# A decoder stack in one kernel: the rotary halves of its keys, its last batch and its two ends rearranged

## The chip, the cores and the metric

The kernel runs on one core of one Trainium2 chip. The metric is the device time of one execution in microseconds (us). Four compute engines and a queue appear in this text: PE (TensorE, matmuls; PEld is its weight load), DVE (VectorE), ACT (ScalarE), POOL (GpSimd), and SP (SyncE), which here only issues transfers.

## What is computed

Six layers in a row on x (8, 256, 128), each followed by `x = _layernorm(x + layer(x))`:

```
L0_attn   windowed self-attention, 16 heads of 8, band of 64, relative bias
L0_xattn  cross-attention, x against ctx_1024 (8, 512, 128), 16 heads of 64
L0_ffn    layernorm, ternary weights, activations rounded to 8 bits
L1_attn   recurrence over 256 steps: state = tanh(state @ A.T + u_t @ B.T) + sp_t
L1_xattn  linear attention with 16 heads of 8, against ctx_1024
L1_ffn    fp8 quantised product with one scale for the whole tensor
```

The change is mostly about one piece of L0_xattn, the keys:

```
k, v = jnp.split(ctx @ Wkv, 2, axis=-1)
x1, x2 = (k[..., :32], k[..., 32:])                   # per head of 64
k = jnp.concatenate([x1 * cos - x2 * sin, x2 * cos + x1 * sin], axis=-1)
attn = softmax(clip(q @ k.T / 8, -11, 11))
```

## The kernel before

Each of the five engines runs its own instruction stream, written out by hand, and waits on semaphores that the others raise. There is no scheduler: the order of the calls in the five `@block` functions is the order on the engines. The order of work is:

**Setup** (to 57.7 us). SP loads all weights. The windowed self-attention of batch 0 runs in full (`first_scores`, `first_turn`, `first_weigh`), and the weights of the cross-attention are split in a high and a low part, so that a product of them takes three matmuls (`split_mm`, L1757 to L1759): ACT makes the high parts (`split_high`), POOL the low ones (`split_low`, L697).

**Eight batches.** A batch is a loop over 8 head pairs p (a pair is two heads of 64, one matmul operand of 128 rows). On PE a pair is two score units of 8 matmuls (`unit`, L2132), the values and the sum of the pair before (`values_of` L2056, `sum_of` L2064), and jobs that prepare later pairs in spare PSUM banks: "keys a", "keys b", "queries", "values 0", "values 1" (`prep_targets`, `number_jobs`; the bank alternates between `bank_p` and `SECOND_BANK[p]`). ACT takes the exponentials of a unit (L1006). DVE clamps them (`clamp`, L1470), takes the reciprocal of the sums and the product for the pair before (`attended`, L1372 and L1373). POOL adds the four quarters of the probabilities (L731, L733, L734) for the sum. Six *slots* per pair hold pieces of the next batch's self-attention, on every engine (`self_attention(b + 1, slot)`).

The keys of pair p + 2 are made thus. PE multiplies `wk_s` ("keys a") and, with weights whose 32-row halves are swapped, `wkx_s` ("keys b"), each with 512 columns of context. DVE multiplies the first bank by `cos_t` into `k_cos` (L1314) at the start of the pair and the second by `sin_t` into `k_sin` (L1316) behind `attended` and the second clamp. POOL adds them into `kr` (`rotate`, L641). `k_cos` has one buffer, so the next key product waits for that addition (`kr_ready`).

**Last batch** (about 711 to 781.5). It has no slots; `beside_last_batch(p)` prepares the FFN and the matrices of the recurrence. Behind it PE runs `output_of_last`, then `sum_of(63)`.

**Transition** (to 815.4). Last norms, quantisation of the FFN's activations (`quantize_f`), the FFN's product, norm (`normalize_x3`), turns of x3 and `begin_z(0)`, `begin_z(1)`, the inputs of the first recurrence steps.

**Recurrence** (255 steps, L2260 on PE and L1055 on ACT). `late_work(t)` puts the rest of the FFN and of the inputs between steps (`LATE_Z = 29`: 27 thirds of a product, one per step from step 29 on), `window(k, i)` the layer L1_xattn for the 16 steps before, `keep_clock` matmuls without use.

**End** (964 to 1021.9). The last windows, the peak of x5 over all tokens, quantisation, the last product and norm. POOL adds the bias there (`add_bias`, L785), DVE normalises (`normalize`, L1189).

Of the kernel before, what the change touches and what calls it, by code (L numbers as in the profile page):

```python
# [28 lines left out]
S = 512  # L29
# [58 lines left out]
def prep_targets(p, last):  # L88

    target = {}  # L90
    if p == PAIRS - 1:
        return {} if last else {"keys a": 1, "values 0": 0, "values 1": 0, "queries": 0, "keys b": 1}
    if p + 2 < PAIRS or not last:
        target["keys a"] = (p + 2) % PAIRS
    target["queries"] = p + 1
    if p + 2 < PAIRS or not last:
        target["keys b"] = (p + 2) % PAIRS
    if p % 2 == 1:
        target["values 0"] = target["values 1"] = (p + 1) // 2
    return target  # L100
# [3 lines left out]
FIRST_JOBS = {("keys a", 0): 0, ("keys b", 0): 0, ("values 0", 0): 0, ("values 1", 0): 0, ("keys a", 1): 1,  # L104
              ("keys b", 1): 1, ("queries", 0): 0}
# [3 lines left out]
def number_jobs():  # L109
# [3 lines left out]
    def add(key, kind, target, second):  # L113
        nonlocal bank
        bank = second if second and bank == "p" else "p"
# [26 lines left out]

SELF_NORMS = 3
# [10 lines left out]
LATE_Z = 29  # L154
HALF_ROWS = P // 2


def n(b, per, k):

    return b * per + k  # L160
# [19 lines left out]
def decoder(nc, a, out):  # L180
    with ExitStack() as ctx:
# [16 lines left out]
        prep_bank = {"p": bank_p, "o0": o0_bank, "d2": bank_d2}  # L198
# [17 lines left out]
        wkx_s = sb("wkx_s", [P, 2, INNER], F32R)  # L216
# [57 lines left out]
        k_cos = sb("k_cos", [P, S])  # L274
        k_sin = sb("k_sin", [P, S])
# [119 lines left out]
        rel_ready = sem("rel_ready")  # L395
        qkv_in = sem("qkv_in")
# [31 lines left out]
        weights_split = sem("weights_split")  # L428
        kv_centred = sem("kv_centred")
# [10 lines left out]
        lat_ready = sem("lat_ready")  # L440
        kr_ready = sem("kr_ready")
# [35 lines left out]
        trig_nat = prob1[:, 6, :].rearrange("p (t k d) -> p t k d", t=2, k=KB)  # L477
# [6 lines left out]
        FIRST_LOADS = 5  # L484
# [3 lines left out]
        def _(sp):  # L488
            loads = {rel_in: 0, qkv_in: 0, first_in: 0, ctx_cols_in: 0, keep_in: 0, split_in: 0, weights_in: 0}
# [13 lines left out]
            load(w_nat[:, 0:3, :], a["L0_attn_w_qkv"].rearrange("(k p) c -> p k c", p=P), signal=qkv_in)  # L503
            load(w_nat[:, 3, :], a["L0_attn_w_proj"], signal=qkv_in)
            sp.dma_start(cb[:, :, :], a["ctx_1024"][0].rearrange("(k p) d -> p k d", p=P)).then_inc(ctx_in, 16)
            load(trig_nat[:, 0], a["L0_xattn_cos"].rearrange("(k p) d -> p k d", p=P), signal=first_in)
            load(trig_nat[:, 1], a["L0_xattn_sin"].rearrange("(k p) d -> p k d", p=P), signal=first_in)
            load(w_l1kv[:, 0:D], a["L1_xattn_wk"], signal=first_in)
            load(w_l1kv[:, D:2 * D], a["L1_xattn_wv"], signal=first_in)
            row("L0_attn_b_proj", b_proj, signal=first_in)  # L510

            sp.wait_ge(d_free, 1)
            sp.dma_start(scratch, rel_row).then_inc(scratch_out, 16)
            col("L0_xattn_ln_ctx_g", CTX_G, signal=ctx_cols_in)
            col("L0_xattn_ln_ctx_b", CTX_B, signal=ctx_cols_in)
            load(keep[:, :, :], a["mask_BxS2_ff1"].rearrange("b (k p) -> p b k", p=P), slow=True, signal=keep_in)
            sp.wait_ge(scratch_out, 16)
            for j in range(G):
                sp.dma_start(bias_mask[:, j:H:G, :], rows(scratch, (1, P), j * SCRATCH, [(G * SCRATCH, G), (1, BAND)])
                             ).then_inc(bias_in[j], 16)  # L520
            load(wkv_nat, a["L0_xattn_Wkv"], signal=split_in)
            load(wq_nat, a["L0_xattn_Wq"], signal=split_in)
            row("L1_xattn_ln_gamma", l1_g)
# [16 lines left out]
            assert loads == {rel_in: 1, qkv_in: 2, first_in: FIRST_LOADS, ctx_cols_in: 2, keep_in: 1, split_in: 2,  # L540
                             weights_in: SETUP_LOADS}, loads

            def load_next(b, src):

# [3 lines left out]
                sp.dma_start(xb[:, :, :], a["x"][src].rearrange("(k p) d -> p k d", p=P)).then_inc(x_in, 16)  # L548

# [7 lines left out]
            for b in range(1, B):  # L557
                load_next(b - 1, b)

            sp.wait_ge(y_full, B - 1)  # L560
            for k, name in ((M_WI, "L1_attn_Wi"), (M_WS, "L1_attn_Ws"), (M_WO, "L1_attn_Wo"), (M_A, "L1_attn_A"),
                            (M_B, "L1_attn_B"), (M_C, "L1_attn_C"), (M_FFN0, "L0_ffn_weight"),
                            (M_FFN1, "L1_ffn_weight")):
                sp.dma_start(mats[:, k, :], a[name]).then_inc(mats_in, 16)

            x4_of_batch = x4_dram.rearrange("k (i b) d -> b k i d", b=B)
            for k in range(1, WINDOWS + 2):
# [26 lines left out]
        def _(pool):  # L594
# [3 lines left out]

            g.memset(ones[:, :], 1.0)
# [4 lines left out]
            g.memset(ident[:, :], 0.0)  # L604
# [3 lines left out]
            g.affine_select(out=ident[:, :], in_=ident[:, :], compare_op=ALU.not_equal, fill=1.0, base=0,  # L608
# [1845 lines left out]
```

## Time and profile before

| | us |
|---|---|
| median of three runs (lowest, highest) | 1025.55 (1023.43, 1025.63) |
| the profiled execution | 1023.58 |
| its span in the profile | 1021.9 |
| setup | 57.7 |
| a steady batch (418.13 to 511.17) | 93.04 |
| the recurrence, one step | 0.567 |
| end, from 964.0 | 57.9 |

| busy in the span | us | share |
|---|---|---|
| PE | 910.6 | 89% |
| DVE | 685.5 | 67% |
| POOL | 510.2 | 50% |
| ACT | 509.7 | 50% |

The profile is one execution. Its times count from the start of the span, which is 1.7 us shorter than that execution's own time. PE's busy time is modelled, and is an average over stages with different limits. The row with the engine's idle time names who ended it.

### The profile page before, as it was taken

To read this page: it belongs to the slowest core of one execution; us is meant where nothing else is said; L and a number is where in the kernel's file an instruction comes from. 1 tells how busy PE (TensorE), PEld (TensorE's weight loads), DVE (VectorE), ACT (ScalarE), POOL (GpSimd) and SP (SyncE) were. 2 spreads that over 40 slices of the span, in tenths; PEclk is the share of its full clock that TensorE was granted. 3 is DMA by queue.
4 is the path that set the end of the run, shared out by engine and by line. 5 is a ranking of instruction groups with operands and counts; after the bars stand their busy time and mean duration, and the time that the engine had idled before them with its cause. 6 is when DMAs were issued, how large, how long until landed. Compare 5 with 4: busy or idle time off the path is not lost.

```text
span 1021.9 us, 22090 instructions
## 1 busy us (share of the span) xinstructions
PE 910.6 (89%) x8504; PEld 646.2 (63%) x8504; DVE 685.5 (67%) x1906; ACT 509.7 (50%) x1441; POOL 510.2 (50%) x642
## 2 busy tenths in 40 slices
PE   6689999999999999999999999998988599999822
PEld 4456666666666666666666666665655389888721
DVE  6457578567767875885678578668788454444477
ACT  6656636653764566366546645663332133333324
POOL 2544475367456644654674466456756112333363
PEclk9999999999999999999999999999989599999955
DMA  7000000000000000000000000000000002212211
GB/s 198 21 6 12 1 2 6 12 1 7 12 1 1 7 11 2 6 2 12 1 6 11 2 1 1 1 2 1 22 0 1 0 12 33 31 29 33 31 13 42
DMA packets 60470, 15.09 MB, mean 15 GB/s; under 512 B 41278, under 2 KB 59726, under 8 KB 60238
## 3 DMA queue, kind: packets, MB, share of 16 engines
q1 hardware_dynamic: 60366, 13.69, 6.3%
q8 instruction: 68, 1.11, 0.4%
q14 instruction: 36, 0.29, 0.1%
HBM read 10.51 MB, written 3.17 MB: 13 GB/s over the span
## 4 chain that ended last, share of the span: by engine, by line
PE 51%; DVE 26%; POOL 11%; ACT 6%; issue 4%; DMA 1%; SPq 0%; POOLq 0%; DVEq 0%; ACTq 0%
PE score_banks L2132 7%; DVE o_rec L1372 7%; PE out_bank L2056 6%; DVE prob L1470 6%; PE bank_a L1752 4%; PE score_banks L2070 4%; PE score_banks L1757 4%; PE score_banks L1788 3%; PE score_banks L2260 3%; POOL psum L733 3%; POOL psum L734 2%; PE bank_d L2273 2%; PE bank_d L1773 2%; PE score_banks L1758 2%; PE score_banks L1759 2%
## 5 line engine op out<-in xcount | busy, mean ns | idle before, releaser
L1006 ACT ACTIVATE prob<-score_banks 128x1024 f32<-128x1024 f32 x128 | 131.1, 1024 | 162.0 <-PE score_banks L2132 161.6
L733 POOL TENSOR_TENSOR psum<-psum,prob 128x512 f32<-128x512 f32 x64 | 81.8, 1278 | 142.1 <-DVE prob L1470 142.1
L2132 PE MATMUL score_banks<-qh,kr 64*128 64x256 f32 x1024 | 146.2, 404 | 2.2 <-ACT qh L915 1.3
L731 POOL TENSOR_TENSOR psum<-prob 128x512 f32<-128x512 f32 x64 | 82.6, 1291 | 92.7 <-DVE prob L1470 92.6
L1372 DVE RECIPROCAL o_rec<-out_bank 128x256 f32<-128x256 f32 x64 | 111.9, 1748 | 24.3 <-PE out_bank L2064 24.3
L2056 PE MATMUL out_bank<-prob,v 128*64 128x256 f32 x1024 | 124.6, 385 | 1.4 <-DVE on L1373 1.4
L2132 PEld LDWEIGHTS score_banks<-qh,kr 64*128 64x128 f32 x1024 | 89.1, 187 | 39.7 <-issue 30.0
L866 ACT ACTIVATE prob<-prob,neg_max 128x128 f32<-128x128 f32 (+1 forms) x256 | 107.2, 427 | 5.1 <-DVE neg_max L1257 5.1
L1470 DVE TENSOR_SCALAR prob<-prob 128x1024 f32<-128x1024 f32 x128 | 101.3, 791 | 12.5 <-ACT prob L1006 12.5
L2056 PEld LDWEIGHTS out_bank<-prob,v 128*64 128x64 f32 x1024 | 67.8, 136 | 46.6 <-issue 17.2
L1055 ACT ACTIVATE prob<-score_banks 128x8 f32<-128x8 f32 x255 | 45.3, 178 | 96.2 <-PE score_banks L2260 96.2
L734 POOL TENSOR_TENSOR psum<-psum,prob 128x512 f32<-128x512 f32 x64 | 81.7, 1277 | 5.0
L641 POOL TENSOR_TENSOR kr<-k_cos,k_sin 128x512 f32<-128x512 f32 x64 | 81.5, 1273 | 4.3 <-DVE k_sin L1316 3.6
L2260 PE MATMUL score_banks<-prob,pt 128*64 128x8 f32 x1020 | 74.3, 210 | 0.6 <-ACT prob L1052 0.3
L1314 DVE TENSOR_TENSOR k_cos<-score_banks,cos_t 128x512 f32<-128x512 f32 x56 | 38.1, 680 | 46.0 <-PE score_banks L1759 28.7
L834 ACT ACTIVATE pt<-bank_a 128x512 f32<-128x512 f32 x84 | 50.2, 598 | 35.5 <-PE bank_a L1752 34.5
L2260 PEld LDWEIGHTS score_banks<-prob,pt 128*64 128x64 f32 x1020 | 53.4, 137 | 21.0 <-ACT prob L1055 14.6
L2070 PE MATMUL score_banks<-w_qkv_t,ident 128*64 128x96 f32 (+1 forms) x336 | 64.9, 277 | 0.0
L1752 PE MATMUL bank_a<-ident,prob 128*128 128x128 f32 x360 | 57.0, 281 | 4.1 <-ACT pt L834 2.3
L1788 PE MATMUL score_banks<-pt,vm 128*32 128x128 f32 x768 | 54.0, 281 | 4.5 <-ACT pt L937 3.8
L1773 PE MATMUL bank_d<-km,q 64*128 64x128 f32 x480 | 49.2, 323 | 9.6 <-DVE row_max L1252 8.3
L759 POOL TENSOR_TENSOR var_eps<-mv,epsilons 128x1 f32<-128x1 f32 x49 | 9.6, 196 | 96.1 <-DVE mv L1574 96.1
(414 smaller groups left out, 2126.3 us busy)
## 6 DMA issues: line engine op xcount, KB each, us to landing
cb<-in_ctx_dram SPq DMA_DIRECT2D x8, 256.0 KB, 2.8
bias_mask<-bias_scratch SPq DMA_DIRECT2D x4, 384.0 KB, 5.4
xb<-in_x_dram SPq DMA_DIRECT2D x8, 128.0 KB, 2.1
prob<-in_L_xattn_Wkv_dram SPq DMA_DIRECT2D x1, 1024.0 KB, 8.1
x_scratch<-v SPq DMA_DIRECT2D x16, 64.0 KB, 1.5
bias_mask<-x_scratch SPq DMA_DIRECT2D x16, 64.0 KB
att_scratch<-on SPq DMA_DIRECT2D x16, 64.0 KB, 1.5
prob<-att_scratch SPq DMA_DIRECT2D x16, 64.0 KB, 3.0
```

The source lines that it names most:

```text
L733: link(g.tensor_tensor(psum[:, p % 2, :], psum[:, p % 2, :], pp[:, 2, :], ALU.add))
L734: g.tensor_tensor(psum[:, p % 2, :], psum[:, p % 2, :], pp[:, 3, :], ALU.add).then_inc(psum_ready, 1)
L866: last = s.activation(pr, pr, ACT.Exp, bias=neg_max[:, qt, j, g:g + 1], accum_out=row_sum[:, qt, j, g:g + 1])
L1006: s.activation(prob[:, p % 2, 2 * u:2 * u + 2, :].rearrange("p k (h q) -> p h k q", h=2), sc[:, 0:2, :].rearrange("p h (k q) -> p h k q", ...
L1372: link(w.reciprocal(o_rec[:, :], bank[:, T:2 * T]))
L1470: w.tensor_scalar(pr, pr, float(np.exp(-CLIP)), float(np.exp(CLIP)), ALU.max, ALU.min).then_inc(clamped, 1)
L1752: return nc.tensor.transpose(out_ap, in_ap, ident[0:in_ap.shape[0], 0:in_ap.shape[0]])
L1788: last = mm(o0_bank[32 * g:32 * g + 32, qt * P:(qt + 1) * P], vm[:, kt, j, 32 * g:32 * g + 32], pt[:, t % 2, i * P:(i + 1) * P], start=(j ...
L2056: mm(o[DH * h:DH * (h + 1), 0:T], v[:, (q // 2) % 2, kb, lo:lo + DH], prob[:, q % 2, kb, T * h:T * (h + 1)], start=(kb == 0), stop=(kb == ...
L2070: mm(bank[0:HALF_ROWS, 0:columns], ident[:, 0:HALF_ROWS], w_qkv_t[:, 0:columns], start=True, stop=True, skip_group_check=True)
L2132: last = mm(sc[:, h, k * T:(k + 1) * T], kr[rows_of, p % 2, kb * P:(kb + 1) * P], qh[rows_of, p % 2, :], start=True, stop=True, skip_group ...
L2260: last = mm(cf[lo:lo + HALF_ROWS, t * B:(t + 1) * B], a_t[:, lo:lo + HALF_ROWS], hid[:, (t - 1) * B:t * B], start=False, stop=True, skip_g ...
```

## The change

**Keys.** "keys b", `wkx_s` and its splits are gone. One bank per key is read twice by DVE: `k_cos` as before, and, right behind the first clamp, `k_raw` = bank x `sin_t` (with the sign of the other half). SP then carries the 32-partition halves of `k_raw` crosswise into `k_sin` with four transfers inside SBUF (`swap_halves`); POOL's `rotate` waits for them. The banks are numbered anew, and SP's loads of the next batch but one stand between these transfers.

```diff
-                    keys_job("a")
+                    keys_job("cos")
                     clamp(0)
+                    keys_job("sin")
                     slots(0, 1)
                     slots(1, 2)
                     if pair >= 1:
                         attended(pair - 1)
                     clamp(1)
-                    slots(2, 3)
-                    keys_job("b")
-                    slots(3, 4)
-                    slots(4, 5)
+                    if pair == B * PAIRS - 1:
+                        add_last_sums()
+                    slots(2, 5)
...
+            def swap_halves(key):
+
+                sp.wait_ge(p_free["dve"], KEYS_DONE[key])
+                if key >= 1:
+                    sp.wait_ge(kr_ready, key)
+                for lo in range(0, P, HALF):
+                    other = lo + HALF if lo % DH == 0 else lo - HALF
+                    sp.dma_start(k_sin[lo:lo + HALF, :], k_raw[other:other + HALF, :]).then_inc(k_swapped, 16)
...
             def rotate(key):
 
-                pool.wait_ge(p_free["dve"], KEYS_DONE[key])
+                pool.wait_ge(k_swapped, SWAPS * (key + 1))
                 g.tensor_tensor(kr[:, key % 2, :], k_cos[:, :], k_sin[:, :], ALU.add).then_inc(kr_ready, 1)
```

DVE, pair 7 of a steady batch, before and after (`o_rec` and `on` are `attended`, `prob` the clamps, `kv_sums` a slot):

```order
L1314 TENSOR_TENSOR k_cos<-score_banks,cos_t 128x512 [waits kr_ready,p_full]
L1470 TENSOR_SCALAR prob<-prob 128x1024 [waits exp_done]
L1296 TENSOR_TENSOR lat_s<-x_t,lat_s 128x256 [waits a_free]
L1372 RECIPROCAL o_rec<-out_bank 128x256 [waits on_ready,o_full]
L1373 TENSOR_TENSOR on<-out_bank,o_rec 128x256 [waits dve_chain]
L1470 TENSOR_SCALAR prob<-prob 128x1024 [waits exp_done]
L1290 COPY kv_sums<-bank_d 128x2 [waits d_full]
L1291 TENSOR_TENSOR kv_sums<-bank_d,l_g 128x128
L1292 SCALAR_TENSOR_TENSOR kv_sums<-l_b,kv_sums 128x128 [waits dve_chain]
L1316 TENSOR_TENSOR k_sin<-score_banks,sin_t 128x512 [waits p_full]
```

```order
L1337 TENSOR_TENSOR k_cos<-score_banks,cos_t 128x512 [waits kr_ready,p_full]
L1520 TENSOR_SCALAR prob<-prob 128x1024 [waits exp_done]
L1343 TENSOR_TENSOR k_raw<-score_banks,sin_t 128x512 [waits k_swapped]
L1319 TENSOR_TENSOR lat_s<-x_t,lat_s 128x256 [waits a_free]
L1420 RECIPROCAL o_rec<-out_bank 128x256 [waits on_ready,o_full]
L1421 TENSOR_TENSOR on<-out_bank,o_rec 128x256 [waits dve_chain]
L1520 TENSOR_SCALAR prob<-prob 128x1024 [waits exp_done]
L1313 COPY kv_sums<-bank_d 128x2 [waits d_full]
L1314 TENSOR_TENSOR kv_sums<-bank_d,l_g 128x128
L1315 SCALAR_TENSOR_TENSOR kv_sums<-l_b,kv_sums 128x128 [waits dve_chain]
```

The sine product moved from behind the second clamp and the slot to a place ahead of the reciprocal, and waits for the last swap (its buffer `k_raw` must have been read).

**Setup.** The identity is made first, the loads of `w_qkv` and `w_proj` go to ACT's queue, the table of the relative bias is stored earlier, sine and cosine later. DVE makes the high parts and the low parts of `wq` and `wv`; POOL keeps the low part of `wk`. The second key comes behind the norm of the latents.

```diff
+            def split_low(part):
+
+                dve.wait_ge(weights_high, part + 1)
+                full, t = ((wq_nat, wq_s), (wkv_nat[:, INNER:2 * INNER], wv_s))[part - 1]
+                w.tensor_tensor(t[:, 1, :], full, t[:, 0, :].bitcast(F32), ALU.subtract).then_inc(weights_split, 1)
```

**Last batch.** Each pair from p = 2 on runs `output_of_last(p - 2)` beside; the matrices are loaded at p == 1. The last pair's two last additions go to DVE; the weights of p == 7 are kept and quantised in the transition.

```diff
+                    def add_last_sums():
+                        dve.wait_ge(last_sum_begun, 1)
+                        dve.wait_ge(clamped, 2 * pair + 2)
+                        link(w.tensor_tensor(psum[:, p % 2, :], psum[:, p % 2, :], prob[:, p % 2, 2, :], ALU.add))
+                        w.tensor_tensor(psum[:, p % 2, :], psum[:, p % 2, :], prob[:, p % 2, 3, :],
+                                        ALU.add).then_inc(last_sum_ready, 1)
...
             values_of(B * PAIRS - 1)
+            sum_of(B * PAIRS - 1)
+            output_of_last(PAIRS - 2)
+            turn_f(B - 2)
+            output_of_last(PAIRS - 1).then_inc(y_full, 1)
...
-            for p in range(PAIRS - 1):
-                output_of_last(p)
-            turn_f(B - 2)
-            sum_of(B * PAIRS - 1)
-            output_of_last(PAIRS - 1).then_inc(y_full, 1)
```

**Transition and recurrence.** Both turns of x3 stand ahead of `begin_z(0)`, in two banks; product 3 and two norms of x3 move into the first windows; late work starts at step 9 instead of 3, its turns at 26 and 58 instead of 17 and 25, and the thirds are spread:

```diff
-LATE_Z = 29
+FIRST_LATE = 9
+Z_EARLY = (13, 14, 15, 22, 30, 38, 42, 43, 44, 45, 46, 54)
+Z_STEPS = [*Z_EARLY, *(t for t in range(64, T) if t % WINDOW_STEPS in (10, 12, 13, 14))][:3 * Z_PARTS]
```

PE in the transition, before and after (`cb` and `k` hold x3 of the first four and the last four batches; L2237 and L2318 are `begin_z`):

```order
L1752 MATMUL bank_a<-ident,cb 128x128 [waits f_t_free,x3_ready]
L1752 MATMUL bank_a<-ident,cb 128x128 x3
L2237 MATMUL score_banks<-prob,pt 128x64x4 [waits ta_free]
L2238 MATMUL score_banks<-prob,pt 128x63x4
L1752 MATMUL bank_a<-ident,k 128x128 [waits ta_free,x3_ready]
L1752 MATMUL bank_a<-ident,k 128x128 x3
L2237 MATMUL score_banks<-prob,pt 128x64x4 [waits ta_free]
L2238 MATMUL score_banks<-prob,pt 128x63x4
```

```order
L1822 MATMUL bank_a<-ident,cb 128x128 [waits f_t_free,x3_ready]
L1822 MATMUL bank_a<-ident,cb 128x128 x3
L1822 MATMUL out_bank<-ident,k 128x128 [waits x3_ready]
L1822 MATMUL out_bank<-ident,k 128x128 x3
L2318 MATMUL score_banks<-prob,pt 128x64x4 [waits ta_free]
L2319 MATMUL score_banks<-prob,pt 128x63x4
L2318 MATMUL score_banks<-prob,pt 128x64x4 [waits ta_free]
L2319 MATMUL score_banks<-prob,pt 128x63x4
```

The second turn, in a bank of its own, went ahead of the first product.

**End.** `window(WINDOWS, 0)` stands ahead of the wait for the last state; the last windows, ACT's copies, DVE's additions and norms and POOL's scalings are put in another order, and POOL's bias additions wait for the peak:

```diff
             pool.wait_ge(x5_ready, 2)
             rstd_of(late, 3, 3, EPS_LN, half=1)
+            pool.wait_ge(red_ready, 3)
             for k in range(4):
                 add_bias(k)
```

## Rows read from the trace of the kernel before

**Rows 1.** Stages (us): busy us (count) of PE, PEld, DVE, ACT, POOL; clock; DMA; GB/s.

```profile
418.13:511.17 93.04, 89.56 (x692) 60.78 (x690) 67.03 (x174) 53.60 (x136) 51.60 (x54) 1.00 0.02 5
...
845.00:964.00 119.00, 119.00 (x2233) 102.14 (x2230) 54.12 (x192) 43.57 (x248) 38.66 (x100) 1.00 0.21 31
```

**Rows 2.** Chain of waits, 418.13 to 511.17: start us, us, what.

```profile
430.50 1.28 POOL kr L641
...
449.97 0.60 DVE k_sin L1316
...
484.80 1.00 ACT prob L1006
```

**Rows 3.** Waits of PE, 418.13 to 511.17: us in all, times, longest.

```profile
PE out_bank L2064 <- POOL psum L734: 1.2, 1, 1.2
```

**Rows 4.** Timeline of DVE: start us, us, operation, [idle before].

```profile
431.87 0.69 DVE L1314 TENSOR_TENSOR k_cos<-score_banks,cos_t 128x512 f32<-128x512 f32 x1 [1.94 <-POOL kr L641]
...
436.14 0.68 DVE L1316 TENSOR_TENSOR k_sin<-score_banks,sin_t 128x512 f32<-128x512 f32 x1
...
469.61 1.76 DVE L1372 RECIPROCAL o_rec<-out_bank 128x256 f32<-128x256 f32 x1 [1.36 <-PE out_bank L2064]
...
473.44 0.45 DVE L1257 TENSOR_SCALAR neg_max<-row_max 128x8 f32<-128x8 f32 x1
```

**Rows 5.** Timeline of PE, pairs 1 and 4.

```profile
447.07 0.51 PE L1757 MATMUL score_banks<-cn_s,wkx_s 128*128 128x512 f32 x1
...
447.89 0.28 PE L1757 MATMUL score_banks<-wv_s,cn_s 128*128 128x256 f32 x1
...
478.77 1.13 PE L2132 MATMUL score_banks<-qh,kr 64*128 64x256 f32 x8
```

**Rows 6.** Queue of SP (issue time), and DMA issues of the page (us to landing).

```profile
970.15 0.32 SPq L574 DMA_DIRECT2D att_scratch<-on  x1
...
x_scratch<-v SPq DMA_DIRECT2D x16, 64.0 KB, 1.5
...
prob<-att_scratch SPq DMA_DIRECT2D x16, 64.0 KB, 3.0
```

**Rows 7.** Waits of PE, 0 to 57.74.

```profile
PE bank_d L1752 <- POOL head_mask L614: 3.1, 1, 3.1
PE score_banks L1757 <- POOL wv_s L697: 2.0, 1, 2.0
```

**Rows 8.** Timeline of PE, last batch and the first us behind it.

```profile
744.09 0.58 PE L1757 MATMUL score_banks<-wv_s,cn_s 128*128 128x256 f32 x1 [1.16 <-DVE k_sin L1316]
...
748.42 2.08 PE L2132 MATMUL score_banks<-qh,kr 64*128 64x256 f32 x8
...
781.40 3.39 PE L2195 MATMUL bank_d<-wo,on 128*128 128x128 f32 x28
...
784.94 0.65 PE L2064 MATMUL out_bank<-psum,ones 128*64 128x256 f32 x4
```

**Rows 9.** Timeline of DVE, last pair of the last batch.

```profile
779.38 0.69 DVE L1470 TENSOR_SCALAR prob<-prob 128x1024 f32<-128x1024 f32 x1
```

**Rows 10.** Timeline of PE, transition.

```profile
811.04 1.06 PE L1752 MATMUL bank_a<-ident,k 128*128 128x128 f32 x4
813.28 1.22 PE L2237 MATMUL score_banks<-prob,pt 128*128 128x256 f32 x2 [1.18 <-ACT prob L989]
```

**Rows 11.** ACT's instruction of a recurrence step (L1055), 815 to 842.

```profile
L1055 ACT ACTIVATE prob<-score_banks x41: 177/178/179, 816.0 to 841.5; 128x8 f32<-128x8 f32 x41
```

**Rows 12.** Timeline of DVE and POOL at the end.

```profile
992.00 0.32 DVE L1577 TENSOR_SCALAR prob<-bias_mask,mv,rstd 128x128 f32<-128x128 f32 x1
...
993.32 3.70 POOL L785 TENSOR_TENSOR x<-prob,b_ffn 128x512 f32<-128x512 f32 x3
993.39 3.71 DVE L1189 TENSOR_SCALAR prob<-bias_mask,mv,rstd 128x128 f32<-128x128 f32 x3 [0.29 <-POOL rstd L626]
```

**Rows 13.** Table of stages for 744 to 751, columns as in rows 1.

```profile
744.00:751.00 7.00, 6.22 (x24) 4.74 (x25) 4.54 (x15) 2.10 (x4) 4.21 (x5) 0.52 0.00 0
```

More of the change, by code:

```diff
@@ L91, in prep_targets @@
     if p == PAIRS - 1:
-        return {} if last else {"keys a": 1, "values 0": 0, "values 1": 0, "queries": 0, "keys b": 1}
+        return {} if last else {"keys": 1, "values 0": 0, "values 1": 0, "queries": 0}
     if p + 2 < PAIRS or not last:
-        target["keys a"] = (p + 2) % PAIRS
+        target["keys"] = (p + 2) % PAIRS
     target["queries"] = p + 1
-    if p + 2 < PAIRS or not last:
-        target["keys b"] = (p + 2) % PAIRS
     if p % 2 == 1:
@@ L111, in number_jobs, with add @@
     jobs, queries_done, keys_done, done, bank, last_of_bank = {}, [], [], {"act": 0, "dve": 0}, None, {}
-    def add(key, kind, target, second):
+    def add(key, kind, target, second, fixed=None):
         nonlocal bank
-        bank = second if second and bank == "p" else "p"
+        bank = fixed or (second if second and bank == "p" else "p")
         engine = "dve" if kind[:4] == "keys" else "act"
@@ L752, in _ @@
             rstd_of_f(B - 1)
-            for k in range(4):
+            for k in range(3):
                 rstd_of(NORMS, k, 4, EPS_LN, half=k % 2)
@@ L1307, in keys @@
             def keys(job, key, part):
-                dve.wait_ge(p_full, job.full)
                 bank = prep_bank[job.bank][:, :]
-                if part == "a":
+                if part == "cos":
+                    dve.wait_ge(p_full, job.full)
                     if key >= 1:
                         dve.wait_ge(kr_ready, key)
-                    w.tensor_tensor(k_cos[:, :], bank, cos_t[:, :], ALU.mult).then_inc(p_free["dve"], 1)
+                    w.tensor_tensor(k_cos[:, :], bank, cos_t[:, :], ALU.mult)
                 else:
-                    w.tensor_tensor(k_sin[:, :], bank, sin_t[:, :], ALU.mult).then_inc(p_free["dve"], 1)
+                    if key >= 1:
+                        dve.wait_ge(k_swapped, SWAPS * key)
+                    else:
+                        dve.wait_ge(sin_kept, 1)
+                    w.tensor_tensor(k_raw[:, :], bank, sin_t[:, :], ALU.mult).then_inc(p_free["dve"], 1)
             def odd_turn(at):
@@ L2061, in sum_of @@
                 q = pair % PAIRS
-                pe.wait_ge(psum_ready, pair + 1)
+                if pair + 1 < B * PAIRS:
+                    pe.wait_ge(psum_ready, pair + 1)
+                else:
+                    pe.wait_ge(last_sum_ready, 1)
                 for h in range(2):
```

426 lines of the change are left out of this document (240 added, 186 removed).

## Prediction

> **What bounds the kernel now.** I read the table of stages first, then, in one steady batch, PE's waits and the chain of waits, and last the timelines of the places that the diff touches. The profiled execution spans 1021.9 us and its own time is 1023.58; every term below is set against that time. The median of the three runs shown is 1025.55, so the execution that I read stands 2 us under it.
>
> The stages [rows 1]: a steady batch (418.13 to 511.17) takes 93.04 us, and seven of the eight batches repeat it. PE is busy for 89.56 of them, which invites the reading that PE sets the batch and that each matmul taken away is time won.
>
> The chain in the steady batch corrects the first reading [rows 2]. From 504 (pair 6) on, over the batch's border and so from 418 again, to 450.6 it runs mostly through DVE and POOL; from 450.6 to 504 it runs through PE, except for a DVE piece at 469.6 to 474.5 and an ACT piece at 484.8 to 489.4. I call the first 40 us **region A** (pairs 6, 7, 0, 1) and the rest **region B** (pairs 2 to 5). PE's waits in a whole batch are only 3.1 us, in six places, the largest 1.2 for POOL's last addition [rows 3], in region A; PE is nearly full there and still is not what the end waits for.
>
> Region A's ring is: key product on DVE, clamp, reciprocal and product of the pair before, second clamp; on POOL two additions and the rotate addition; then the next key product, which waited 1.94 us for POOL [rows 4]. `k_sin` at 436.14 lies beside the POOL additions, off that ring [rows 4]. Only at pair 1 (449.97) is it on the chain [rows 2].
>
> **The change, part by part.**
>
> *Key matmuls.* Each of 64 keys loses three 128x512 matmuls. From the first one's start to the next job's start is 447.89 - 447.07 = 0.82 us of PE [rows 5]. In region A (half of the keys) PE would only wait longer: nothing. In region B four keys could give 3.3 us; but at pair 2 the following scores wait for DVE's row maxima, at pair 3 the turn behind the job waits for the exponentials of maxima that end at 473.9, at pair 4 the ACT piece decides [rows 2, 4]. I take 0 + 0.2 + 0 + 0.5, that is -0.7, and keep 3.3 as the other end.
>
> *`k_raw` ahead of the reciprocal.* The sine product keeps its 0.68 us (0.60 from start to start), but it now stands right behind the first clamp, ahead of the slots and of `attended`, so it is on the ring in all four pairs of region A: +2.4. The `k_sin` that it replaces was on the chain once, at pair 1, and PE had other work up to 451.5: -0.1. In region B DVE has idle time before the reciprocal (1.36 us at 469.61 [rows 4]), which hides it; without that cover it would be 4 x 0.6 more.
>
> *Transfers.* Four issues of 32 partitions x 2 KB. An issue occupies the queue 0.32 us; 64 KB to or from DRAM land 1.5 us after issue with 512-byte rows, 3.0 with small pieces [rows 6]. So the last quarter lands between 3 x 0.32 + 1.5 = 2.5 and 3 x 0.32 + 3.0 = 4.0 us after the product. From the end of `k_raw` to the place of the rotate addition there are, besides the attended pair (2.1) and the clamp (0.6), two POOL additions of 1.28: 5.3 us. Cost 0; if the cover failed, POOL would wait and the ring with it. SP carries nothing else in a batch but the two loads of the next but one, moved to pairs 1 and 4 behind these transfers; each is needed most of a batch later. The Trainium skill, DMA: Bandwidth & Descriptors, section Anatomy of one DMA, gives about 2.0 us of fixed cost per DMA, mostly the receipt of the write; by it the last quarter would land at 0.96 + 2.0 + 0.15 = 3.1 us, and the sum would be the same.
>
> So a steady batch: +2.4 - 0.1 - 0.7 = +1.6; seven of them **+11.2**. Ends: -3.3 (region B pays in full, the product hides) and +4.7 (neither cover nor gain in region B).
>
> *Setup.* PE waited 3.1 us for POOL's masks and 2.0 for POOL's low half of `wv` [rows 7]. The identity now comes first, and DVE takes the splits of `wq` and `wv`, with ACT free of them. Two key jobs go (1.6). 3.1 + 2.0 + 1.6 = 6.7, less one sine product ahead of the projection (0.6): **-6**. Ends 0 (DVE, which took the work, becomes the bound) and -9.
>
> *Last batch.* At pair 3 PE waited 1.16 us for `k_sin` and then ran at half clock, so that a score unit took 2.08 us [rows 8]; elsewhere it takes 1.13 [rows 5]. The value job can now follow `queries` without the key job and that wait (-0.8, -1.2), and the unit may keep its clock (-0.9): **-3**, ends 0 and -5. At the end 28 output matmuls (3.39 us at 781.40) stood before the last sum (784.94) [rows 8]. They move into the pairs; the last two additions go to DVE: the second clamp ends at 780.0 [rows 9], and 780.0 + 2 x 0.68 = 781.4, where the values end too. So the sum starts at 781.4 instead of 784.9: -3.5, and the weights' quantisation, now behind the norms, costs 0.7 of that: **-2.8**, ends 0 and -4.
>
> *Transition.* The second turn of x3 started at 811.04 behind the first begin_z, and its product at 813.28 [rows 10]. With both turns issued up front in two banks this difference goes: **-2.3**, ends -1 and -3.
>
> *Recurrence.* 40 steps took 841.5 - 816.0 = 25.5 us [rows 11]; the 119 us up to 964 [rows 1] hold the last 210 steps or so, 0.567 each: 2.8 too much. Part of it is the clock coming back, part DVE and POOL work that PE waits for, which now comes later: **-1.7**, ends +1 (late products spread over more steps) and -3.
>
> *End.* DVE's normalisation of three tiles took 3.71 us beside three of POOL's bias additions, 3.70 [rows 12]. The first tile of its kind takes 0.32 by itself: 3.71 - 3 x 0.3 = 2.8 less. The last windows' new order I value at another 2.2, from the waits of its chain; POOL's four additions now stand beside the quantisation, where I charge 1. **-4**, ends +1 and -6. No row shows DVE's quantising products beside such additions. The Trainium skill, SBUF - State Buffer, section SBUF: two separate sides, calls the port pair that DVE and GpSimd share an exclusive lock, held for the whole instruction, also against DVE operations with two SBUF inputs; the 3.71 us for three tiles agrees with it. By that rule, several of the four moved additions would hold up the quantisation for 1.24 each, up to +4.9 in place of my +1, and the end would gain nothing.
>
> **Sum**: 11.2 - 6 - 3 - 2.8 - 2.3 - 1.7 - 4 = -8.6, so 1023.6 - 8.6 = **1015.0 us**.
>
> **The rivals.**
>
> *PE's relief pays (chance 0.2).* Region B gives its 3.3 us and the sine product hides: 7 x -3.3 = -23; with -19.8 from the other places 1023.6 - 43 = 981. For: PE is busy for 89.56 of 93.04 us [rows 1]. Against: the DVE and ACT pieces in the chain, and the 1.94 us that DVE waited for POOL [rows 4], which no matmul touches.
>
> *The clock falls in region A (0.15): slower.* Region A's PE loses 4 x 0.82 of work while the ring grows by 2.4 us, so its idle time there grows by 5.7 us a batch. In the last batch a wait of 1.16 us [rows 8] stood right before 7 us at a granted clock of 0.52 [rows 13], near the lower of the two levels, 1.2 of 2.4 GHz. If each batch had one such stretch, PE would do in 7 us what took 3.6: +3.4 a batch, +24, giving 1015 + 24 = 1039. It decides from 1.2 us a batch on (8.6 over 7 batches). Against it: the batch's granted clock is 1.00 now with 3.1 us of waits [rows 1, 3]. The Trainium skill, TensorE: Matmul & The Clock Gate, Part 1, says that the clock is throttled by default and that activity releases it; more idle time pushes that way, as in the 0.52 stretch.
>
> *The ends give half (0.12).* Setup, last batch and end are full of short waits of which the next is always near: -9.9 instead of -19.8, 1023.6 + 11.2 - 9.9 = 1024.9, no change.
>
> *The transfer isn't hidden (0.03).* If four quarters took over 5.3 us, the rotate addition would be late by the excess in each pair of region A; at 1 us that is 4 x 7 = +28, 1043. The slow end of [rows 6] speaks against it.
>
> *My forecast (0.5)*: the ring grows a little, the ends more than pay.
>
> **How the numbers follow.** A measurement of this kernel can tell about 0.2% (2 us) from no change. The first rival is faster (0.20). Of the forecast 0.45 is faster and 0.03 the same, 0.02 slower; the third rival gives 0.03, 0.07 and 0.02; the second and fourth are slower (0.18). Faster 0.68, same 0.10, slower 0.22. The forecast's own range goes halfway to the batch's two ends, 7 x -0.85 and 7 x 3.15 around 1023.6 - 19.8: 998 to 1026. The whole range reaches on into the first rival below and the second above until 2 in 10 are left out: 986 to 1036.
>
> **What would show it.** Right: steady batches of 94 to 95 us; on DVE a `k_cos` that waits for POOL in pairs 0, 1, 6 and 7; swaps that land 2.5 to 4 us after `k_raw` and before POOL comes to them; PE's busy time down by 6 us a batch and its waits up by more; PEclk 1.00 throughout. Wrong: a batch under 92 us (first rival), or a clock under 0.98 in region A (second).

## The result, and the profile after

The changed kernel takes 1033.22 us (median of five runs, 1031.93 to 1035.74) against 1025.33 for the kernel before in the same comparison: 1.0087 times the time, with an interval of 1.0068 to 1.0106. It is slower, where 1015 was forecast. The profiled execution is the one of 1033.22, with a span of 1031.5, 9.6 us over the span before.

First the page of the changed kernel: PE's busy time, and the granted clock in 40 slices.

```profile
PE 881.5 (85%) x8358; PEld 629.2 (61%) x8358; DVE 688.3 (67%) x1913; ACT 505.1 (49%) x1434; POOL 502.1 (49%) x637
...
PEclk9989999999899999999999999899899789999965
```

PE has 29 us less to do than before (910.6) and the kernel is longer. The slices of 8 among the nines from 258 us on have no counterpart inside the seven steady batches of the kernel before.

The table of stages, cut where the reciprocal of a batch's first pair begins (columns as in [rows 1]); the fifth and sixth batch repeat the third and fourth:

```profile
73.64:168.64 95.00, 84.21 (x666) 56.80 (x666) 67.74 (x174) 53.43 (x137) 51.30 (x53) 1.00 0.12 27
168.64:263.67 95.03, 84.33 (x667) 56.81 (x666) 67.74 (x176) 53.52 (x137) 51.33 (x53) 1.00 0.12 27
263.67:361.67 98.00, 88.05 (x667) 59.70 (x666) 67.09 (x176) 53.62 (x137) 51.29 (x53) 0.95 0.11 27
361.67:458.24 96.57, 85.90 (x667) 57.87 (x666) 67.72 (x176) 53.63 (x137) 51.29 (x53) 0.98 0.12 27
...
652.78:751.98 99.20, 87.71 (x645) 59.88 (x644) 64.10 (x161) 47.04 (x121) 49.28 (x50) 0.91 0.12 28
751.98:807.19 55.21, 49.13 (x364) 32.57 (x363) 49.15 (x93) 21.59 (x32) 38.77 (x38) 1.00 0.11 25
...
834.37:979.60 145.23, 145.00 (x2751) 129.71 (x2752) 67.28 (x239) 52.26 (x298) 43.84 (x112) 1.00 0.18 28
979.60:1031.50 51.90, 16.65 (x189) 11.48 (x185) 39.18 (x140) 18.82 (x43) 27.62 (x54) 0.58 0.15 31
```

| stretch | before | after | difference |
|---|---|---|---|
| to the first reciprocal | 73.64 | 73.64 | 0.0 |
| batches 1, 2 | 93.0 each | 95.0 each | +4.0 |
| batches 3 to 6 | 93.03 each | 98.00, 96.57, 97.96, 96.58 | +17.0 |
| batch 7 | 91.62 | 99.20 | +7.6 |
| last batch | 62.24 | 55.21 | -7.0 |
| transition | 29.73 | 27.18 | -2.6 |
| recurrence | 148.53 | 145.23 | -3.3 |
| end | 58.0 | 51.9 | -6.1 |

Two things are in the batches. One is there in all seven, at a clock of 1.00: +2.0. The other comes in batches 3 to 7 only, together with a lower clock. The table of stages for two stretches of batch 3, and PE's timeline in the first:

```profile
267.67:274.67 7.00, 7.00 (x33) 4.77 (x33) 2.61 (x11) 4.24 (x15) 2.72 (x3) 0.53 0.00 0
335.67:339.67 4.00, 4.00 (x23) 3.28 (x20) 4.00 (x5) 2.35 (x4) 2.31 (x2) 0.57 0.00 0
```

```profile
267.60 1.44 PE L1843 MATMUL bank_d<-km,q 64*128 64x128 f32 x8 [1.97 <-DVE row_max L1275]
...
270.55 2.08 PE L2224 MATMUL score_banks<-qh,kr 64*128 64x256 f32 x8
```

PE waits 1.97 us for DVE's row maxima and then runs at the lower level: the score unit that took 1.13 [rows 5] takes 2.08. It is what [rows 8] and [rows 13] showed once in the last batch before. From batch 2 to batch 3 the step between the reciprocals around this stretch grows by 2.95 us (10.72 to 13.67), and no other step of the batch by more than 0.02: the second low stretch, 4 us at 0.57, cost nothing.

The chain of waits in batch 2 of the changed kernel, from pair 6 to pair 1:

```profile
227.98 0.60 DVE k_raw L1343
...
240.19 0.60 DVE k_raw L1343
...
241.83 1.68 DVE o_rec L1420
...
247.28 1.28 POOL kr L680
...
248.65 0.14 DVE k_cos L1337
...
249.94 0.60 DVE k_raw L1343
250.54 1.68 DVE o_rec L1420
...
262.09 0.68 DVE k_raw L1343
```

`k_raw` (0.60 to 0.68) is a piece of the chain ahead of each of these four reciprocals, as forecast. The rotate addition that the next `k_cos` waited for is one too, but DVE waits for it only once in this batch (2.5 us, in pair 0; before 1.9), not in all four pairs. DVE's waits for it, over the whole kernel (before: 17.3 us, 11 times):

```profile
DVE k_cos L1337 <- POOL kr L680: 30.6, 12, 4.7
```

The transfers, 88 of them between 236 and 500 us: issue (ns, least, median, most), and the time to landing.

```profile
L574 SPq DMA_DIRECT2D k_sin<-k_raw x88: 507/590/1377, 240.8 to 499.5; - x88
...
DMA to landing us min/median/max: 1.9/2.0/3.6
```

An issue takes 0.59 us, not 0.32 as in [rows 6]; a landing 2.0. Between the product and the last landing lie some 3.8 us, and in the batches POOL never waited for them.

At the end of the kernel:

```profile
1004.34 0.85 DVE L1212 TENSOR_SCALAR prob<-bias_mask,mv,rstd 128x128 f32<-128x128 f32 x3
...
1006.13 5.11 POOL L828 TENSOR_TENSOR x<-prob,b_ffn 128x512 f32<-128x512 f32 x4 [2.05 <-DVE small L1748]
...
1008.95 1.16 DVE L1768 TENSOR_SCALAR v<-prob 128x512 uint32<-128x512 uint32 x1
1010.15 1.63 DVE L1772 SCALAR_TENSOR_TENSOR prob<-v,prob 128x512 f32<-128x512 f32 x1
...
1012.43 0.42 DVE L1768 TENSOR_SCALAR v<-prob 128x512 uint32<-128x512 uint32 x1
1012.88 0.69 DVE L1772 SCALAR_TENSOR_TENSOR prob<-v,prob 128x512 f32<-128x512 f32 x1
```

DVE's normalisation of three tiles takes 0.85 instead of 3.71 [rows 12]; in its place two quantising operations on DVE take 1.16 and 1.63 us beside the four bias additions, where the same two on the next tile, with POOL done, take 0.42 and 0.69.

### The profile page after: what moved, and what is told of

It is laid out like the page before. It is cut to its first block, busy times and chain, and to the rows that moved or that the text cites. A ratio compares the mean times of both kernels' runs of the same rounds, so it can differ in the third digit from the quotient of the medians.

```text
span 1031.5 us, 22102 instructions
## 1 busy us (share of the span) xinstructions
PE 881.5 (85%) x8358; PEld 629.2 (61%) x8358; DVE 688.3 (67%) x1913; ACT 505.1 (49%) x1434; POOL 502.1 (49%) x637
## 4 chain that ended last, share of the span: by engine, by line
PE 47%; DVE 27%; POOL 11%; ACT 9%; issue 5%; DMA 1%; POOLq 0%; DVEq 0%; SPq 0%; ACTq 0%
PE score_banks L2224 7%; DVE o_rec L1420 7%; DVE prob L1520 6%; PE out_bank L2133 5%; PE bank_a L1822 3%; PE score_banks L2343 3%; PE score_banks L2150 3%; PE score_banks L1858 3%; POOL psum L774 3%; ACT prob L1028 3%; PE bank_d L1843 2%; PE bank_d L2356 2%; ACT prob L911 2%; POOL psum L775 2%; PE score_banks L1827 2%
## 5 line engine op out<-in xcount | busy, mean ns | idle before, releaser
L2224 PE MATMUL score_banks<-qh,kr 64*128 64x256 f32 x1024 | 153.5, 420 | 11.9 <-ACT qh L960 6.8
L774 POOL TENSOR_TENSOR psum<-psum,prob 128x512 f32<-128x512 f32 x63 | 80.1, 1272 | 160.7 <-DVE prob L1520 160.7
L2224 PEld LDWEIGHTS score_banks<-qh,kr 64*128 64x128 f32 x1024 | 93.4, 194 | 47.7 <-issue 37.7
L1520 DVE TENSOR_SCALAR prob<-prob 128x1024 f32<-128x1024 f32 x128 | 105.1, 821 | 9.4 <-ACT prob L1028 9.4
L775 POOL TENSOR_TENSOR psum<-psum,prob 128x512 f32<-128x512 f32 x63 | 80.1, 1272 | 4.9
L1337 DVE TENSOR_TENSOR k_cos<-score_banks,cos_t 128x512 f32<-128x512 f32 x49 | 33.6, 687 | 67.1 <-PE score_banks L1829 36.5
L1843 PE MATMUL bank_d<-km,q 64*128 64x128 f32 x480 | 52.2, 337 | 19.7 <-DVE row_max L1275 17.6
L2343 PEld LDWEIGHTS score_banks<-prob,pt 128*64 128x64 f32 x1020 | 51.3, 134 | 16.0 <-ACT prob L1077 8.5
L2150 PE MATMUL score_banks<-w_qkv_t,ident 128*64 128x96 f32 (+1 forms) x336 | 60.7, 264 | 0.0
L1822 PEld LDWEIGHTS bank_a<-ident,prob 128*128 128x128 f32 x360 | 39.3, 140 | 34.6 <-ACT pt L879 21.0
```

What stands on the lines that cost most here:

```text
L774: link(g.tensor_tensor(psum[:, p % 2, :], psum[:, p % 2, :], pp[:, 2, :], ALU.add))
L775: g.tensor_tensor(psum[:, p % 2, :], psum[:, p % 2, :], pp[:, 3, :], ALU.add).then_inc(psum_ready, 1)
L1520: w.tensor_scalar(pr, pr, float(np.exp(-CLIP)), float(np.exp(CLIP)), ALU.max, ALU.min).then_inc(clamped, 1)
L1822: return nc.tensor.transpose(out_ap, in_ap, ident[0:in_ap.shape[0], 0:in_ap.shape[0]])
L2150: mm(bank[0:HALF_ROWS, 0:columns], ident[:, 0:HALF_ROWS], w_qkv_t[:, 0:columns], start=True, stop=True, skip_group_check=True)
L2224: last = mm(sc[:, h, k * T:(k + 1) * T], kr[rows_of, p % 2, kb * P:(kb + 1) * P], qh[rows_of, p % 2, :], start=True, stop=True, skip_group ...
```

## The experiments

All twelve were run beside the kernel before, which had medians of 1023.4, 1026.0 and 1025.0 us in the three sets. Batches are cut as above.

**PE's idle time filled (e1_warm).** In the changed kernel (the added argument makes the job's matmuls run twice):

```diff
-                    prep("keys", prep_keys)
+                    prep("keys", prep_keys, not last and p in (0, 1, PAIRS - 1))
...
-                        prep("values 0", prep_values, 0)
+                        prep("values 0", prep_values, 0, not last and p == 1)
```

> The changed kernel, with work for PE put back where it idles: the key job of pairs 7, 0 and 1 and the first value job of pair 1 are computed twice into the same bank (about 3 us a batch, results unchanged). Theory 1 (the clock: two parts of the loss, +2.0 us a batch of ring and some 14 us of half clock in batches 3 to 7): all seven steady batches take 95 to 95.5 us at a granted clock of 1.00, total 1019 to 1023. Theory 2 (the ring alone, the low clock costs nothing since DVE and POOL decide there): batches as before this edit, 95 to 98, total 1032 to 1036. Theory 3 (PE's work is what counts): more work makes it slower, 1040 and more.

Measured: 1020.22 us (1018.37 to 1021.57), 0.9961 of before (0.9945 to 0.9978). Batches 3 and 7:

```profile
264.78:359.88 95.10, 86.77 (x685) 59.37 (x681) 67.82 (x176) 53.60 (x137) 51.39 (x53) 1.00 0.12 27
...
645.15:740.36 95.21, 84.67 (x660) 57.73 (x656) 64.75 (x160) 47.66 (x122) 49.33 (x50) 0.98 0.12 29
```

PE computes more and the kernel is shorter. The seven batches take 665.8 us together instead of 678.3, 12.6 less. The medians differ by 13.0, but they are from two sets; each against the kernel before beside it (+7.9 and -3.2) makes 11.1. Theory 1 holds: all seven batches take 95.08 to 95.21, six of them at a clock of 1.00 and the seventh at 0.98. Batches 1 and 2, which were at 1.00 without the added matmuls too, take 0.1 more with them, so it is the clock that the others got back. The low clock cost 11 to 13 us, and this kernel, nearly without it, is 0.4% faster than the one before.

**The sine product back behind the second clamp (e2_late).**

```diff
                     clamp(0)
-                    keys_job("sin")
...
                     clamp(1)
+                    keys_job("sin")
                     slots(2, 5)
```

> The changed kernel with the sine product moved back behind the second clamp, so that it is off the DVE part of the ring, and its transfers start 2.6 us of POOL additions ahead of the rotate addition. Theory 1 (ring): -2.4 us a batch from DVE; but issue of four transfers at 0.59 plus 2.0 of landing is 3.8 us, so POOL waits about 1.5 to 2 us for the swap in each pair, and gives back +1.5 x 3 to 4 pairs: a batch of 96 to 99, and POOL's waits for the transfers near 64 instead of 2. Theory 2 (the transfers are hidden anywhere): a batch of 93 or less, total 1010 to 1018.

Measured: 1114.41 us, 1.0879 of before (1.0813 to 1.0946); a batch of 105 to 109. The waits of POOL in the whole kernel, and those of PE in batch 2:

```profile
POOL kr L680 <- DMA k_sin<-k_raw: 108.0, 58, 4.6
```

```profile
PE score_banks L1827 <- DVE k_raw L1343: 12.0, 4, 4.3
```

Both theories missed. POOL waits for the swap in nearly every pair, 1.9 us in the mean, as computed. I had left out the second effect: the bank is now read twice, so a late product holds it, and PE's next job waits 12 us a batch for that. The granted clock of this batch is 0.92, so a part of its growth is clock.

**Two buffers for `k_cos` and `k_sin` (e3_two).**

```diff
-        k_cos = sb("k_cos", [P, S])
+        k_cos = sb("k_cos", [P, 2, S])
...
-                    if key >= 1:
-                        dve.wait_ge(kr_ready, key)
+                    if key >= 2:
+                        dve.wait_ge(kr_ready, key - 1)
```

> The changed kernel with two buffers each for k_cos and k_sin, so that a key product no longer waits for POOL's rotate addition of the pair before. Theory 1 (ring through k_cos): DVE's wait for the rotate addition (30.6 us in all) goes, a steady batch falls to 91 to 93 us, PE's gaps shrink and the clock stays at 1.00, total 1000 to 1012. Theory 2 (the ring is not closed by the buffer but by the order on POOL or by ACT): a batch stays at 95 and the total within 1 per cent of the changed kernel.

Measured: 1009.51 us, 0.9853 of before (0.9832 to 0.9874). Batches 2 and 4:

```profile
169.35:262.61 93.26, 84.05 (x667) 56.73 (x666) 68.30 (x176) 53.52 (x137) 51.72 (x53) 1.00 0.12 28
...
357.42:452.29 94.87, 86.39 (x667) 58.54 (x666) 68.31 (x174) 53.66 (x137) 51.71 (x53) 0.96 0.12 28
```

The wait of `k_cos` for POOL is gone from DVE's waits, and where the clock stays up a batch takes 93.26 instead of 95.03. That is 1.8 us, a little short of the 91 to 93 expected, and the clock still falls in other batches. The step that shrinks is the one between the reciprocals of DVE's pairs 7 and 0, where the wait was (8.70 to 6.65 us); the next one grows by 0.3. The kernel beats the one before, though it keeps the change whole. Which of the two buffers does it was not tried apart.

**Only what lies behind the batches (e4_tail).** The kernel before, with the changed last batch, transition, recurrence and end.

> The kernel before, with only the parts of the change behind the steady batches: outputs and last sums inside the last batch, both turns of x3 first, late work spread, the new order at the end; keys, banks of the seven batches and setup as before. Theory 1 (parts add up): last batch -4 to -7, transition -2.5, recurrence -3.2, end -6.1, so 1025.3 - 17 = 1006 to 1010. Theory 2 (they gained only what the slower batches had pushed out): 1015 to 1025.

Measured: 1005.86 us, 0.9823 of before (0.9802 to 0.9844). Batch 2 and the last batch:

```profile
167.10:260.06 92.96, 89.53 (x692) 60.77 (x690) 66.99 (x176) 53.54 (x137) 51.48 (x54) 1.00 0.02 6
723.45:779.42 55.97, 52.93 (x382) 35.77 (x381) 52.43 (x94) 22.12 (x32) 39.88 (x39) 1.00 0.01 4
```

-17.5 us against the kernel before in the same set, as theory 1 wanted: the gain of the ends in the changed kernel (-19.0 in the table) was real, and the seven batches are as before (92.96 against 93.03).

**Both (e5_two_warm)**, the edits of e1_warm and e3_two together.

> The doubled matmuls of e1_warm and the two buffers of e3_two together. Theory 1 (clock and ring add up; the two-buffer run had its batches at 93.3 where the clock stayed up): all steady batches 93.3 us, clock 1.00, so 1.5 less than e3_two in four of seven batches and the stretch in pair 0: total 1001 to 1006. Theory 2 (the two-buffer kernel is bound by PE, and more PE work costs it): 93.3 + 3 a batch, total 1020 and more.

Measured: 1006.61 us, 0.9824 of before (0.9798 to 0.9850).

```profile
260.44:354.00 93.56, 86.46 (x683) 59.26 (x681) 68.31 (x174) 53.56 (x137) 51.80 (x53) 1.00 0.12 28
```

Ring and clock add up, nearly: 93.57 in the first six batches (0.3 over e3_two's best, the price of the added matmuls), and a clock of 1.00 in all eight. The total lies just over theory 1's range.

**The ends and two buffers, without the change to the keys (e6_tail_two).**

> e4_tail with two buffers each for k_cos and k_sin, so the keys by two matmul jobs as in the kernel before. Theory 1 (the ring through k_cos is what holds region A): DVE's 17.2 us of waits for the rotate addition go, -1.5 to -2.0 a batch as in e3_two, total 992 to 996. Theory 2 (with the second key job PE is the next bound at once): batches stay at 92.0 to 93.0, total 1003 to 1006.

Measured: 998.70 us (998.43 to 1001.70), 0.9746 of before (0.9723 to 0.9770), the lowest time of all the versions.

```profile
258.76:350.99 92.23, 89.37 (x694) 60.69 (x692) 67.09 (x174) 53.55 (x137) 51.97 (x54) 1.00 0.02 5
```

The second buffers give 0.7 us a batch here (92.96 in e4_tail), less than theory 1 wanted, with PE busy for 89.4 of 92.2. The batch is where theory 2 put it, the total lies between the two theories.

**The sine product shortened (e7_short).** In e1_warm; the sine half of the keys is left out for 448 of 512 columns:

```diff
-                    w.tensor_tensor(k_raw[:, :], bank, sin_t[:, :], ALU.mult)
+                    w.tensor_tensor(k_raw[:, 0:64], bank[:, 0:64], sin_t[:, 0:64], ALU.mult)
```

> e1_warm with the sine product on 64 of its 512 columns (the other columns of k_raw stay zero, so the sine half of the keys is left out there); the transfers are as before. Theory 1 (the sine product lies on the ring in four pairs, and is the batch's growth): 0.68 becomes 0.1 to 0.2, a steady batch falls from 95.1 to 92.8 to 93.2. Theory 2 (the batch grew by something else, the transfers or the banks): a batch of 94.5 to 95.1.

Measured: 999.59 us, 0.9746 of before (0.9723 to 0.9769).

```profile
258.58:351.07 92.49, 86.48 (x685) 59.31 (x683) 63.13 (x174) 53.46 (x137) 51.64 (x54) 1.00 0.12 28
```

The product takes 0.216 instead of 0.682 us, and the batch falls by 2.6, to 92.5. Four times 0.466 is 1.9; the steps between reciprocals shrink by 0.47, 1.18, 0.46 and 0.46 in DVE's pairs 6, 7, 0 and 1, the whole of region A, and by nothing in sum elsewhere. Region A is then as long as in the kernel before (43.98 us against 43.94). The growth of the batch is the sine product's place, not the transfers, which ran as before.

**More work for PE in setup (e8_setup).** The value jobs and the second key job ahead of the first score unit are computed twice.

> The changed kernel with the value jobs and the second key job of setup computed twice (1.4 + 1.4 + 0.8 us of PE more before the first score unit, results unchanged). Theory 1 (setup gained 3.9 us and the half clock right behind it took them back): the granted clock in 48 to 64 us stays at 1.00, the first reciprocal starts at 70 to 71.5 instead of 73.64; later batches as in the changed kernel. Theory 2 (the first pairs are held by the slots, whatever the clock): it stays at 73.6 or comes later by the added 1 to 3 us.

Measured: 1033.56 us, 1.0088 of before (1.0059 to 1.0116). The stretches from 52 us to the first reciprocal, in this kernel and in the changed one:

```profile
52.00:64.00 12.00, 8.16 (x46) 5.43 (x46) 7.24 (x20) 5.06 (x10) 5.88 (x7) 1.00 0.19 42
64.00:72.21 8.21, 7.01 (x43) 4.06 (x43) 3.61 (x14) 5.57 (x12) 4.88 (x7) 0.79 0.08 22
72.21:84.46 12.25, 10.04 (x69) 6.97 (x71) 9.34 (x36) 6.70 (x21) 5.05 (x4) 0.86 0.10 23
```

```profile
52.00:64.00 12.00, 10.64 (x39) 7.14 (x41) 5.21 (x13) 4.46 (x9) 4.46 (x5) 0.57 0.19 43
64.00:73.64 9.64, 6.94 (x52) 4.10 (x48) 5.00 (x21) 6.18 (x14) 6.22 (x8) 1.00 0.06 18
73.64:84.36 10.72, 8.51 (x69) 5.80 (x71) 9.77 (x35) 6.58 (x21) 5.06 (x4) 1.00 0.11 24
```

The clock stays up until 64 us and falls behind that (0.79, and 0.86 up to the second reciprocal). The first reciprocal comes at 72.21 instead of 73.64, the second at 84.46 instead of 84.36. Neither theory: the fall was postponed, not prevented. The 1.4 us at the first reciprocal can't be told from chance: e10_less_b has the instructions of the kernel before up to pair 2, and its first reciprocal came at 76.21 against 73.64, with a granted clock of 0.72 between 46 and 58 us.

**PE relieved in the kernel before (e9_less, e10_less_b).** The second key job is one matmul of 64 columns, in all pairs of the seven steady batches or in their pairs 2 to 5; the sine half of the keys is left out for the other columns.

```diff
+                if light:
+                    mm(bank[:, 0:64], wkx_s[:, 0, c], cn_s[:, b % 2, 0, 0:64], start=True, stop=True).then_inc(p_full, 1)
+                    return
```

> The kernel before, with the second key job of every pair of the seven steady batches cut to one matmul of 64 columns (0.82 us becomes 0.1; the sine half of the keys is left out for the other columns). All other engines do what they did. Theory 1 (PE's relief gives little in region B and lowers the clock in region A): a batch is 92.3 where the clock stays at 1.00 and 93 to 96 where it falls, total 1018 to 1035. Theory 2 (the matmuls set the batch): -0.7 x 8 = -5.8 a batch, total 985 or less.

> As e9_less, but the second key job is cut only in pairs 2 to 5 (region B). Theory 1 (the scores and ACT hold pairs 2 and 4, so that four jobs of 0.7 give 0.7 together, and region A keeps its matmuls and its clock): a batch of 92.2 to 92.6, clock 1.00, total 1019 to 1022. Theory 2 (each matmul of region B counts in full): a batch of 90.2, total 1004.

Measured: 1022.46 us (0.9985 of before, 0.9969 to 1.0002) and 1022.57 (0.9988, 0.9973 to 1.0003). Batches 1 and 2 of e9_less, then batch 3 of e10_less_b:

```profile
73.24:165.73 92.49, 85.35 (x678) 58.08 (x674) 66.90 (x174) 53.57 (x138) 51.51 (x54) 1.00 0.02 5
165.73:259.54 93.81, 86.67 (x676) 59.22 (x674) 66.51 (x176) 53.55 (x137) 51.53 (x54) 0.98 0.02 6
```

```profile
261.29:353.82 92.53, 87.20 (x684) 59.53 (x682) 66.88 (x174) 53.45 (x137) 51.54 (x54) 1.00 0.02 5
```

A batch falls from 93.03 to 92.49 with eight jobs cut and to 92.53 with the four of region B: the four of region A are worth nothing, those of region B 0.5 us where PE's busy time fell by 2.4 (89.56 to 87.20). Two batches of e9_less took 1.3 and 1.6 us more, the first of them shown above, at a clock of 0.98; e10_less_b, which keeps region A's matmuls, lost none.

**The rotate addition in the next pair (e11_next, e12_next_early).** e5_two_warm with POOL's `rotate` behind the first addition of the next pair; in e11_next the sine product is also behind the second clamp.

```diff
                     link(first)
+                    if pair >= 1:
+                        rotate(pair + 1)
                     pool.wait_ge(clamped, 2 * pair + 2)
```

> e5_two_warm with the sine product behind the second clamp again, and POOL's rotate addition moved into the next pair, behind its first addition, where POOL waits for the second clamp: the transfers then have most of a pair. Theory 1 (the place of the sine product on DVE is what costs, once the transfer is hidden): POOL no longer waits for swaps, a batch falls from 93.6 to 91 to 92.5, total 990 to 1000. Theory 2 (the late sine product holds its bank, and PE's next job waits for it): 93.5 to 97, total 1006 to 1030.

> As e11_next, but with the sine product at its place in the changed kernel, so that against e5_two_warm only POOL's rotate addition is moved. Theory 1 (with two buffers the rotate addition decides nothing): a batch of 93.3 to 93.8, total 1004 to 1008; the difference to e11_next is then the price of the sine product's place. Theory 2 (the moved addition delays POOL's sums, which PE waits for): 94 to 96.

Measured: 1102.19 us (1.0769 of before, 1.0736 to 1.0801) with batches of 105.8, and 1038.48 (1.0131, 1.0089 to 1.0173) with 99.0. PE's waits in batch 2, of e11_next and of e12_next_early:

```profile
PE score_banks L1827 <- DVE k_raw L1343: 5.9, 3, 2.5
PE score_banks L2226 <- POOL kr L680: 4.3, 1, 4.3
```

```profile
PE score_banks L2226 <- POOL kr L680: 4.9, 1, 4.9
```

And the stage row of that batch of e12_next_early:

```profile
169.99:269.03 99.04, 89.00 (x684) 61.20 (x683) 66.51 (x176) 53.56 (x137) 52.30 (x54) 0.95 0.11 26
```

Failures both, but telling. e12_next_early is 5.4 us a batch worse than e5_two_warm: PE's score unit waits 4.9 us for `kr` once a batch, a wait that neither theory had. Its clock is 0.95, so how much of the 5.4 is the wait and how much the clock is not shown. e11_next adds 6.8 more at a clock of 0.94, and no pair waits for a swap in the batches: the late sine product is the only edit between the two, and PE's waits for `k_raw` (5.9 us) name the bank it holds.

## Why the prediction was wrong

- **The clock, the step that failed.** The forecast put the price of lower PE activity at 0 and gave "the clock falls in region A" a chance of 0.15, on the ground that the clock stood at 1.00 with 3.1 us of waits a batch. That evidence was from a PE with 3.5 us idle a batch; the change leaves it 10.8. The measured price is 11 to 13 us (e1_warm against the changed kernel). The rival's mechanism and place were right (a wait of 1.97 us for the row maxima at pair 1, then 7 us at 0.53); its size was not: 3.4 a batch in all seven was assumed, and 3.0, 1.5, 3.0, 1.5 and 4.0 in five of them came (each against 95.0, the last against the 95.21 of e1_warm). The measured time lies inside the stated range only because that range reaches up into this rival; the forecast itself had the sign wrong.
- **The ring, right in sum, in part by luck.** +1.6 a batch was worked out, +2.0 measured at a clock of 1.00. From the reciprocals of batch 2 in both kernels, region A grew by 2.57 and region B shrank by 0.55. The terms were +2.3 for the sine product's place in region A (e7_short gives back 2.6) and -0.7 for the key matmuls (-0.5 by e9_less and e10_less_b, none of it in region A). But the +2.4 was four times 0.6, and the four steps grew by 0.10, 1.32, 0.57 and 0.58. The forecast also had `k_cos` wait for POOL in four pairs; it waits in one. And the chain of the kernel before holds the product at pair 3 of region B too, in a row that no term counts:

```profile
473.88 0.60 DVE k_sin L1316
```

- **The first rival, PE's relief pays, fell.** Region B gives 0.5 of its 3.3 us, and the gain sits where the forecast put 0.5 of its 0.7, behind the job of pair 5.
- **The transfers, right.** 3.8 us from product to landing against bounds of 2.5 to 4.0, and no wait of POOL in a batch. The issue was mis-sized, 0.59 for 0.32, inside these bounds. The fixed cost of about 2.0 us that the prediction takes from the Trainium skill (DMA: Bandwidth & Descriptors, Anatomy of one DMA) is stated there for transfers issued by GpSimd; these went through SP's queue and landed 2.0 us after issue. The cover holds only at this place: e2_late.
- **Setup, wrong.** -6 was forecast. The first score unit came at 53.88 instead of 57.74, -3.9, and at the first reciprocal both kernels stand at 73.64. The first two score units of the changed kernel take 2.08 us each, at a clock of 0.57 in 52 to 64 us; the kernel before had 0.81 in 52 to 58 and 1.00 behind it. That the half clock took all 3.9 back fits but is not shown: between executions the first reciprocal of unchanged setup code moved by 2.6 us (73.64 and 76.21), so that the 0 is itself uncertain by so much.
- **The ends, right in sign and too small**: -3 and -2.8 for the last batch, -2.3, -1.7 and -4 make -13.8; measured -7.0, -2.6, -3.3 and -6.1, -19.0. The end's quantisation costs 1.9 us beside POOL where I charged 1: three of DVE's operations take 0.3, 0.7 and 0.9 us longer. The lock of the Trainium skill (SBUF - State Buffer, SBUF: two separate sides), taken for all four additions, would have made it 4.9; the trace shows less than half, and no operation that is longer by a whole addition of 1.28. Which of the reordered parts gave more than forecast was not tried one by one.

In the sum: 11.2 of ring became 15.6 (six times 2.0, and 3.6 in batch 7), 0 of clock became 13.0, -6 of setup became 0, -13.8 of ends became -19.0. That is +9.6, the difference of the spans. The split between ring and clock is loose: the 95.21 of batch 7 in e1_warm is itself at a clock of 0.98, so a part of its 3.6 is clock and not ring: with two buffers and a clock of 1.00 (e3_two) batch 7 takes 91.58, as before the change. It is luck that the ends gave 5.2 more than forecast, nearly as much as setup gave less.

## What to carry to other kernels

Work taken from an engine that is full but not waited for gives its idle time back as a risk: ask what the clock does with it, before counting the gain as zero. When a product moves from a later to an earlier place on an engine, follow the ring that it enters, and look for the single buffer that closes it: the second buffers of `k_cos` and `k_sin` were worth 1.8 us a batch in the changed kernel and 0.7 in the one before, where eight removed matmul jobs gave 0.5. A low clock cost time here only where PE's work decided: of the two stretches in batch 3 the one in pair 1 cost 2.95 us, and the one in pair 7, where the chain runs through DVE and POOL, nothing. And a change of many parts deserves to be split: its ends alone were worth 1.8%, which its middle hid.

## What was not expected of the hardware

Seven microseconds of half clock followed a wait of 1.97 us in batches 3, 5 and 7 but not in 1 and 2, whose timelines up to there are the same to 0.1 us: which of them is hit differs. Batches 4 and 6 lost 1.5 us behind the same wait, to a shorter stretch. Whether the spread of the five runs (1031.9 to 1035.7) comes from this is not shown: their mean clocks are 0.936 to 0.944, and the run of 1034.8 has the highest of them. PE's idle time alone does not tell either: 7.1 us a batch left the clock at 1.00 in e5_two_warm and let it fall in two batches of e9_less. An issue of a transfer inside SBUF took 0.59 us on SP's queue, where one of SBUF to DRAM took 0.32. What exactly in PE's activity decides was not tried; it stays open.
